# Four tap products of a causal convolution on ScalarE, added by VectorE: one layer of GCN, Mamba and a routed FFN on one Trainium2 core

## The reference

```python
h = relu(adj @ layernorm(x) @ gcn_w + gcn_b);  h = layernorm(h) * ln_g + ln_b
xc, z = split(h @ w_in)                              # 256 channels each
xconv = sum(xpad[k:k+L] * conv_w[:, k] for k in range(4)) + conv_b
u = silu(xconv)
dbc = u @ w_xp;  dt = softplus(dbc[:, :8] @ w_dt + b_dt);  B, C = the rest of dbc
state = exp(dt * A) * state + dt * B * u             # scan over 8192 rows, 256 x 16 states
y = (sum over the 16 states of state * C + u * D_skip) * silu(z)
x = x + y @ w_out
H = gelu(layernorm(x) @ W1 + b1)
out = x + prob * (H @ Wd[expert] + bd[expert])       # expert = argmax of the gate
```

## Time and profile before

| | before |
|---|---|
| median of 3 runs | 1661.06 us (1660.46 to 1665.43) |
| profiled execution, its own time | 1657.32 us |
| span in that profile | 1655.3 us |
| VectorE busy | 1513.2 us (91%) |
| TensorE busy | 1412.5 us (85%) |
| ScalarE busy | 959.3 us (58%) |
| GpSimd busy | 795.4 us (48%) |
| DMA | 279 GB/s over the span |
| granted TensorE clock, mean | 0.94 |

### The profile page before, as it was taken

The page is one execution under the profiler, slowest core; times in us unless marked ns, Lnnn a source line. Parts: engine busy times, 40 slices in busy tenths (PEclk is TensorE's granted clock), DMA queues, the critical chain, the costliest instruction groups (busy, mean ns, idle before and its releaser), DMA issues. The chain is left out here.

```text
span 1655.3 us, 16767 instructions
## 1 busy us (share of the span) xinstructions
PE 1412.5 (85%) x4265; PEld 689.9 (42%) x4265; DVE 1513.2 (91%) x1928; ACT 959.3 (58%) x1829; POOL 795.4 (48%) x411
## 2 busy tenths in 40 slices
PE   5999999899889999899999989989999985444578
PEld 4743333343333544344443434444444433132354
DVE  9297898999999999999999999999999999999953
ACT  3363555374727476675848475666748474756551
POOL 0043243645344455555545545555555555557541
PEclk9999999999999999999999999999999997656789
DMA  9899988889888899889898888889988895425730
GB/s 304 256 319 322 337 310 303 294 292 357 304 324 308 316 316 332 317 299 320 296 329 291 307 314 299 299 300 318 313 303 298 302 311 203 161 95 163 223 96 18
DMA packets 173733, 462.18 MB, mean 279 GB/s; under 512 B 20095, under 2 KB 67826, under 8 KB 173380
## 3 DMA queue, kind: packets, MB, share of 16 engines
q1 hardware_dynamic: 123586, 309.76, 53.6%
q10 hardware_dynamic: 44994, 139.48, 24.8%
q0 software_dynamic: 5056, 11.87, 1.9%
HBM read 445.75 MB, written 18.17 MB: 280 GB/s over the span
## 5 line engine op out<-in xcount | busy, mean ns | idle before, releaser
L540 POOL TENSOR_TENSOR h_c<-hidden,bc_ring 128x1024 f32<-128x1024 f32 (+1 forms) x272 | 605.2, 2225 | 788.2 <-DVE inject L1177 616.4
L1318 PE MATMUL ps_adj<-ring,nodes 128*128 128x512 f32 x1920 | 883.0, 605 | 59.5 <-DMA ring<-adj 37.2
L1082 DVE TENSOR_TENSOR_SCAN hidden<-decay,state,inject 128x512 f32<-128x512 f32 (+1 forms) x544 | 632.4, 1204 | 34.9 <-ACT decay L646 10.2
L1318 PEld LDWEIGHTS ps_adj<-ring,nodes 128*128 128x128 f32 x1920 | 359.0, 192 | 523.9 <-issue 387.8
L646 ACT ACTIVATE decay<-dt_sb,negA 128x512 f32<-128x512 f32 (+1 forms) x544 | 348.0, 688 | 46.8 <-issue 23.1
L1177 DVE TENSOR_TENSOR inject<-dtu_sb,bc_ring 128x1024 f32<-128x1024 f32 (+1 forms) x272 | 316.6, 1164 | 4.7 <-DMA bc_ring<-bc_dram 3.8
L1128 DVE TENSOR_TENSOR y_sum<-y_sum,h_c 128x1024 f32<-128x1024 f32 (+1 forms) x238 | 276.0, 1160 | 7.5 <-POOL h_c L540 4.5
L638 ACT COPY state<-hidden 128x2 f32<-128x2 f32 x271 | 52.1, 192 | 357.9 <-DVE hidden L1082 356.3
L511 POOL DMA_INDIRECT out<-o_sb,out_at x68 | 99.6, 1465 | 51.5 <-DVE o_sb L971 38.9
L506 POOL DMA_INDIRECT bins<-rec,dest x60 | 89.6, 1494 | 11.7 <-issue 9.8
L1314 PE MATMUL ps_adj<-ring,nodes 128*128 128x256 f32 x256 | 60.9, 395 | 19.1 <-DVE nodes L891 17.3
(11 more groups left out here) (216 smaller groups left out, 1355.7 us busy)
## 6 DMA issues: line engine op xcount, KB each, us to landing
ring<-adj SPq DMA_DIRECT2D x480, 512.0 KB
bc_ring<-bc_dram ACTq DMA_DIRECT2D x240, 512.0 KB
wd_ring<-wd_rows SPq DMA_DIRECT2D x64, 288.0 KB, 3.5
ring<-adj SPq DMA_DIRECT2D x64, 256.0 KB
bc_ring<-bc_dram ACTq DMA_DIRECT2D x32, 256.0 KB
got<-bins SPq DMA_DIRECT2D x60, 129.0 KB, 3.2
nodes<-x_rows ACTq DMA_DIRECT2D x8, 512.0 KB, 8.9
x_tile<-x_rows SPq DMA_DIRECT2D x16, 256.0 KB, 7.1
```

The lines of the kernel that those rows point to most:

```text
L540: nc.gpsimd.tensor_tensor(h_c[:, s % 2, :, 0:w], hidden[:, s % 2, :, 0:w], over_halves(bc_ring[:, s % BC_RING, 1], w), ALU.mult).then_inc( ...
L1082: scan = nc.vector.tensor_tensor_scan(hidden[:, s % 2, h, 0:w], decay[:, s % 2, h, 0:w], inject[:, h, 0:w], state[:, h, s:s + 1], ALU.mult ...
L1318: last = nc.tensor.matmul(ps_adj[:, 0], nodes[:, m], ring[:, g % RING, m % GROUP], start=(m == 0), stop=(m == J - 1))
```

## The change

In the bodies 5 to 14 (by_scalar) the three later taps are made as bare products by ScalarE, two activations of 512 elements each (tap_product), into buffers that are free then: tap 1 into dt_sb[:, p] in slot 7, tap 2 into soft in slot 8, tap 3 into front_ab (front_a and front_b, now one tile) in slot 8. VectorE adds them to u_sb with three tensor_tensor of 1024 elements, one in slot 7 and two in slot 8. The table STEADY takes the place of the identity in these bodies: the stage f[8] (Silu of u and z, and the product with w_xp) moves from slot 8 to slot 9, and f[9] (the copies rows_sb and low_sb, their DMA, and the product with w_dt) from slot 9 to slot 10. The other bodies keep their code.

```diff
+STEADY = (0, 1, 2, 3, 4, 5, 6, 7, 9, 10, 10, 11, 12, 13, 14, 15)
...
-        front_a = sb("front_a", [P, T])
-        front_b = sb("front_b", [P, T])
+        front_ab = sb("front_ab", [P, 2, T])
+        front_a, front_b = front_ab[:, 0], front_ab[:, 1]
...
@@ scalar
+            def tap_product(dst, k):
+                for h in range(2):
+                    tap = nc.scalar.activation(dst[:, h], conv_in[:, h, k:k + T], ACT.Identity,
+                                               scale=vec("conv_w", TAPS * h + k))
+                tap.then_inc(tap_ready, 1)
...
-                f = FRONT.get(i, range(SLOTS))
+                f = FRONT.get(i, STEADY if by_scalar(i) else range(SLOTS))
...
+                    if by_scalar(i) and s == 7:
+                        st.wait(dtu_ready, 0, 0)
+                        tap_product(dt_sb[:, p], 1)
+                    if by_scalar(i) and s == 8:
+                        c.wait(h_done, -1, 4)
+                        tap_product(soft, 2)
+                        st.wait(xz_done, 1, 4)
+                        tap_product(front_ab, 3)
@@ vector (and the same change of f)
+                    if by_scalar(i) and s in (7, 8):
+                        own = Count(dve, i - 5)
+                        for k, product_of in ((1, dt_sb[:, p]),) if s == 7 else ((2, soft), (3, front_ab)):
+                            if k == 1:
+                                st.wait(conv_first, 1, 2)
+                            st.wait(conv_step, 1, 2 * (k - 1))
+                            own.wait(tap_ready, 0, k)
+                            nc.vector.tensor_tensor(u_sb[:], u_sb[:], product_of[:], ALU.add).then_inc(conv_step, 2)
-                    if front and s == f[7]:
+                    if front and not by_scalar(i) and s == f[7]:
...
@@ tensor (the same change of f)
```

More of the change, by code:

```diff
@@ L278, in gnn_mamba_moe @@
         conv_first, conv_step = sem("conv_first", 2), sem("conv_step", 2 * (TAPS - 1))
+        tap_ready = sem("tap_ready", 3)
         u_ready, dbc_done = sem("u_ready"), sem("dbc_done")
```

## The result

The changed kernel takes 1674.48 us, the median of seven runs (1670.31 to 1677.27), beside 1663.16 us for the kernel before in seven (1660.46 to 1665.43). The ratio is 1.0064, with a 95% interval of 1.0044 to 1.0083: slower by 11.3 us, where 27 were forecast. The range on record, 1667 to 1714, holds it; the forecast's size is wrong by more than a factor of two.

What follows compares the result with a forecast made beforehand. VectorE, busy 91% of the span, was taken to bound the kernel. 10 x (-0.38 + 1.3 + 0.8 + 1.0) = +27 us on 1657.3 gives 1684, and 3.7 more for the median 1688 us; range 1667 to 1714.

Steps and rivals of the forecast that it cites:

- VectorE's saving: On VectorE's list three additions replace six operations, 3.60 us for 3.98: 0.38 us saved in a body.
- ScalarE's chain: ScalarE's steps from the first tap on, product pairs at 1.24 us: decay 10 ends 1.65 us later in body 12.
- The wait at scan 10: VectorE waits for the later decay 10 ahead of scan 10: 1.0 us in body 12, 1.3 us in the mean.
- H: End of TensorE's hidden products, counted from the start of ScalarE's u pair; tap 2 waits for it; 6.16 us in body 12.
- The second thin place: Between decays 10 and 13 ScalarE's two copies make VectorE wait again: 0.8 us a body, of 0 to 1.3.
- TensorE, moved and not made longer: TensorE idles for u, multiplies low_sb later, and leaves 1.0 us per body not made up, of 0 to 2.85.
- The signs: What the profile after would show: bodies of 93.5 to 96 us, four table loads, VectorE idle before scans 10 and 13.
- Rival 1: TensorE closes the loop: a body takes 96.3 us, 4.5 more, +42 us in all, 1703 us; chance 0.25.
- Rival 2: The cover holds: VectorE waits for nothing and keeps its saving, -3.8 us, 1657 us; chance 0.06.
- Rival 3: Each switch of ScalarE's tables costs 1.4 us more than its load, in ten bodies, 1702 us; chance 0.03.

Runs made afterwards that it cites:

- stage not moved: The changed kernel with the identity in place of STEADY, products still on ScalarE, Silu back in slot 8; 1696.78 us, ratio 1.0192 to the kernel before.
- groups moved: The changed kernel with two of TensorE's adjacency groups taken from slot 11 to slot 9 from body 7 on; 1677.86 us, ratio 1.0093.
- reordered kernel: The tap behind the decay, with the Exp load between Gelu and Silu left out and decay 13 ahead of dt's Exp and Ln; 1658.44 us.
- tap behind the decay: The changed kernel with tap 2 made into front_ab, then decay 9, only then the wait for hidden products and tap 3 into soft; 1665.12 us.
- one load less: The changed kernel without the table load for Exp between Gelu and Silu; 1675.58 us, ratio 1.0057 to the kernel before.

## Why the forecast was right in its way and wrong in its size

- *VectorE's saving*: 0.38 a body forecast, 0.39 measured.
- *ScalarE's chain*: the pair at 1.24, the one load more, 14.97 us from tap 2's start to decay 10: right (ScalarE is ready for tap 2 at 5.1 us behind the u pair's start, 5.5 in the working), and the kernel with the stage not moved confirms that VectorE pays what exceeds its slack, to 0.2 us.
- *The wait at scan 10*: 1.3 forecast, 1.0 measured. The working took H from the kernel before, 6.5 in the mean of its later value with ScalarE's; in the changed kernel's trace the same mean is 6.1. A first long wait in body 5 (4.37 us at H = 8.37) is followed by four bodies with H at 5.4 to 6.6. The working had 3.2 us for body 5 by its H; the 1.1 us more are the late start of the u pair.
- *The second thin place*: 0.8 forecast, 0.45 measured. I let only a part of ScalarE's small idle times between decays 10 and 13 pay for the two copies. In body 12 decay 13 ends 15.04 us behind decay 10, and the forecast had 15.9. In the changed kernel it is 15.24 to 15.41 in five bodies, where the idle time paid nearly all, 15.8 to 16.8 in the bodies 5 to 7, and 17.24 in the bodies 8 and 12, where the gate's logits are late and VectorE waits for them ahead of scan 13.
- ***TensorE, moved and not made longer*, is the step that failed.** It said that 1.0 us of its 2.85 us delay would not be made up in a body, 10 us in all. All was made up: in the bodies 6 to 13 the hidden products end 38.8 us behind the body's mark in the mean, and 39.2 before the change. TensorE's waits over the bodies 7 to 14 before the change were

```profile
PE ps_f L1230 <- ACT low_sb L752: 17.2, 8, 3.6
PE ps_f L1230 <- ACT u_sb L736: 13.7, 6, 6.9
PE ps_adj L1318 <- ACT front_a L672: 13.0, 6, 2.5
```

  With the change the wait for u grew to 43.8 us, and the ones for low_sb (5.7) and for the front's copy (3.8) shrank. The groups moved into its idle time bring nothing, and with ScalarE reordered they bring 1 us. Without this term the forecast would have been +17 us. Three microseconds less at scan 10 and 3.5 less at scan 13 leave +10.5, and the gate's 3.5 make it 14, for 13.8 by the marks and 11.3 by the medians. So the +17 would have been near the result in part by luck: a wait that was left out makes up for half of what two others were put too high.
- *What the forecast left out*: the gate's reduction waits for its logits in bodies 8 and 12, 3.5 us. TensorE's lower clock behind its idle time is in both, as the slow product of low_sb shows; the working had the lower clock as the upper bound of the wait at scan 13 (1.3), and no wait ahead of the gate.
- *The signs*: bodies of 93.5 to 96 us were forecast, and two of ten are (8 and 12); one is 97.3 and seven are 91.6 to 92.9. The six tap rows, the four loads, TensorE's wait for u and the waits at scans 10 and 13 came as forecast.
- Rival 1, the closed loop, has fallen with the same step, although the idle time of 4.6 us and the lower clock that spoke for it were there. Of its signs, tap 2 waited for TensorE in every body, but the wait at scan 10 was over 3 us in body 5 alone, and the second wait was there. Rival 2 did not happen, but the reordered kernel is its case. Rival 3 fell: loads end 0.01 us before the next activation (1275.02 + 1.28 and 1276.31), and leaving one out made the chain to decay 10 shorter by 1.42 us, where the rival had 2.7 (the load and 1.4 more): its 1.28 us, and 0.14 by which two activations without a load between them follow closer.
- The working did not see the kind of the dependence. It used H as ten fixed numbers. H changes from body to body in every trace here, the one before included (3.8 to 8.4), and was harmless there, since ScalarE needed the hidden products behind both Silus only. The change made each microsecond of it beyond 5.1 a wait of VectorE. The tap behind the decay shows this: 9 us for moving one wait behind one pair of exponentials.

What makes H late can be read from the traces, though no run isolates it. Take the bodies 6 to 13 of all thirteen traces, 104 bodies, and the granted clock from each mark to the end of the hidden products. It is 1.00 in 78 bodies and 0.96 in 26. H is 7.0 or more in 24 of the 26, and in three of the 78. Bodies 11 and 12 of the kernel with the groups moved, with H = 8.37 and 5.95 (columns of the earlier trace rows):

```profile
1136.44:1177.91 41.47, 38.38 (x101) 18.09 (x100) 40.47 (x47) 23.28 (x58) 23.90 (x13) 0.96 0.89 309
1231.25:1270.14 38.89, 36.96 (x101) 17.22 (x100) 37.64 (x45) 23.43 (x58) 23.42 (x12) 1.00 0.91 326
```

So a stretch at the lower clock ahead of the hidden products stands beside nearly every late end. What makes the clock fall there in one body and not in the next stays open, and so does why the gate is late in the bodies 8 and 12 alone and why the kernel with one load less met four late bodies. No kernel was run that makes ScalarE's chain longer by a known amount and changes nothing else.

## What to carry to other kernels

When work goes to an engine with much idle time in the mean, look at each thing that it must hand over and how long before its use, and count every wait that the new work brings in ahead of it. A wait for another engine's result carries that engine's jitter with it: put it behind what the bound engine needs next, and choose the buffers so that this can be done. An idle stretch gained on a third engine is not a loss as long as its other waits shrink by as much; look then at what it hands over just behind the stretch (here the gate's logits).

## What was not expected of the hardware

TensorE's clock fell in each body behind 4.62 us of idle time (11.48 in body 14; the product of u took 3.26 to 3.78 us for 1.98), and this did not lengthen the bodies by itself, except where logits were late. A lower clock ahead of the hidden products, which the kernel before has too, is what goes with the long waits at scan 10. And the start of body 5, behind 570 us of the same code, varies by 10 us between executions (565.1 to 575.2 in thirteen traces), about as much as the change costs: two profiles can't be compared by their spans here, only by marks around the part that changed.
